# Two softmax attentions: the residual added by TensorE through the identity matrix, the sum copied into x by ScalarE

## Chip, cores and metric

The kernel runs on one core of one Trainium2 chip. The metric is the device time of one execution in microseconds; lower is better. Time before is the median of three runs.

## What is computed

Four transformer layers on x of shape (16, 64, 128), each an attention and a feed-forward part, each with a layer norm in front and a residual add behind. The change touches the attention of layer 0 and that of layer 3. Both are, cut to what matters:

```python
q, k, v = LN(x) @ Wq.T + bq, ctx @ Wk.T + bk, ctx @ Wv.T + bv     # 16 heads of 8
attn = softmax(q k.T / sqrt(8) [+ bias, masked, in layer 3], axis=-1)
x = x + ((attn @ v) @ Wo.T + bo)
```

Behind layer 0's attention comes a mixture of experts (`moe0`), behind layer 3's a quantised feed-forward part (`ffn3`). Each begins with the layer norm of the new x.

## The kernel before

The 1024 tokens are eight tiles of 128. x lies in SBUF as `x_tm` (128 partitions of tokens, tile, 128 features), in float32, for the whole kernel. Every engine runs its own instructions in the order of the program text; semaphores tie the engines together. A piece of text under `@block.scalar` is appended to ScalarE's queue, and so on, so what stands later in the text on the same engine runs later on it.

`attention` (line 449) serves both layers (`masked` is true in layer 3). Its loops run over a step t, with the tiles staggered:

- TensorE (lines 560 to 577), step t: scores of tile t+1 (16 matmul records, line 525) into PSUM banks 0 to 3; transposes of the probabilities of tile t-1 (line 539); values weighed by the probabilities of tile t-2, and the sums of the probabilities (lines 552 and 556); the output projection of tile t-3 (line 576) into bank 7. In layer 3 the values come ahead of the transposes. The values of tile j wait until `o_fm` of tile j-1 is written, the projection of tile j until `o_fm` of tile j is written and until x has taken tile j-1 (`y_added`), as both use bank 7.
- ScalarE (lines 581 to 592), step t: the exponential of tile t, and two copies of the transposed probabilities of tile t-1 from PSUM (line 591). It has nothing to do in the last steps.
- VectorE (lines 611 to 667), step t: reads the scores of tile t (layer 0: maximum, line 636, and difference, line 639; layer 3: scale, bias and maximum, lines 623 to 629); reciprocal of the sums and product into `o_fm` for tile t-3 (lines 656 and 658, in layer 3 also 653 and 654); the add of the projection of tile t-4 into `x_tm` (line 664); the norm's statistics of tile t-5 (line 245).
- GpSimd adds the row bo to all of x once (line 501, in layer 3 line 601), and in layer 3 takes the maximum off the scores (line 605).

The few lines around the projection and the add:

```python
pe.wait_ge(of_ready, j + 1)
if j >= 1:
    pe.wait_ge(y_added, j)
PE.matmul(ps[:, 7, 0:128], o_fm[:, j * P:j * P + P], mat(wo), start=True, stop=True)\
    .then_inc(y_ready, 1)
...
dve.wait_ge(y_ready, j + 1)
V.tensor_tensor(x_tm[:, j], x_tm[:, j], ps[:, 7, 0:128], ALU.add).then_inc(y_added, 1)
```

After the loop of layer 0, ScalarE's queue holds two operations for layer 1 (line 1022, 128x1024 each), and then those of the layer norm: a dummy square root that brings its table in (line 281), the square root of the variance (line 283), which waits for VectorE's statistics (lines 263 and 265), and three of the eight normalised tiles (line 286). After the loop of layer 3 the layer norm follows at once. The layer norm's transposes on TensorE (line 309) wait for the normalised tiles.

SP's queue issues the transfers. `rest_in` counts eleven of them and is waited for only as a whole (`REST`); the transfer of `wq8` is one of them. The weights of layer 2's experts (`moe2_in`, four transfers) go out after layer 0, the mask and bias of layer 3 (`bias_in`, three transfers) after layer 2's attention.

Of the kernel before, what the change touches and what calls it, by code (L numbers as in the profile page):

```python
# [114 lines left out]
def build(nc, A, out):  # L115

    ctx = ExitStack()
    with ctx:
# [109 lines left out]
        V4_CLEAR, KV_CLEAR, AB_CLEAR, V4_CLEAR_AGAIN = 1, 2, 3, 4  # L228

        table, table_set = sb("table", [P, 2]), sem("table_set")  # L230

        @block.gpsimd
        def _(pool):
            G.memset(table[:], 1.0).then_inc(table_set, 1)
            G.memset(v4[:], 0.0).then_inc(cleared, 1)
# [11 lines left out]
        def layernorm(feature_major=True, between=None):  # L247
# [29 lines left out]
            @block.scalar  # L277
            def _(act):
                if n == 0:
                    act.wait_ge(table_set, 1)  # L280
                AC.activation(table[:, 1:2], table[:, 0:1], ACT.Sqrt)
                act.wait_ge(stat_ready, n + 1)
                AC.activation(rstd[:], rstd[:], ACT.Sqrt).then_inc(std_ready, 1)  # L283
                act.wait_ge(shift_ready, n + 1)
                for j in range(ON_DVE, NT):
                    ins = AC.activation(h_tm[:, j, :], x_tm[:, j, :], ACT.Identity, bias=shift[:, j:j + 1],
                                        scale=rstd[:, j:j + 1])
                ins.then_inc(h_rest, 1)
                if between is not None:
                    between(act)  # L290
                if feature_major:

                    for k in range(2):
                        act.wait_ge(tr_ready, 2 * nf + k + 1)
                        AC.activation(h_fm[:, 512 * k:512 * k + 512], ps[:, 4 + k, :], ACT.Copy)\  # L295
                            .then_inc(hf_ready, 1)
# [152 lines left out]
        def attention(n, layer, wq, wo, bo, prepared, masked, bm_ready=None):  # L449
# [56 lines left out]
            def _(pe):  # L506
# [54 lines left out]
                for t in range(NT + 3):  # L561
# [9 lines left out]
                    if 0 <= t - 3 < NT:  # L571
                        j = t - 3
                        pe.wait_ge(of_ready, j + 1)
                        if j >= 1:
                            pe.wait_ge(y_added, j)
                        PE.matmul(ps[:, 7, 0:128], o_fm[:, j * P:j * P + P], mat(wo), start=True, stop=True)\
                            .then_inc(y_ready, 1)

            @block.scalar
            def _(act):  # L580
                for t in range(NT + 2):
# [3 lines left out]
                    if 0 <= t - 1 < NT:  # L585
# [3 lines left out]
                        for k in range(2):  # L589
                            act.wait_ge(ptT_ready, 2 * j + k + 1)  # L590
                            AC.activation(pT[j % 2][:, 512 * k:512 * k + 512], ps[:, 4 + k, :], ACT.Copy)\  # L591
                                .then_inc(pt_ready, 1)

# [14 lines left out]
            def _(dve):  # L608
                if masked:
                    dve.wait_ge(bm_ready, NT)  # L610
                for t in range(NT + 5):
# [47 lines left out]
                    if 0 <= t - 4 < NT:  # L659
                        j = t - 4  # L660
                        if j == 0 and not masked:
                            dve.wait_ge(bo_added, 1)
                        dve.wait_ge(y_ready, j + 1)
                        V.tensor_tensor(x_tm[:, j], x_tm[:, j], ps[:, 7, 0:128], ALU.add).then_inc(y_added, 1)
# [318 lines left out]

        @block.sync
        def _(sp):
            sp.dma_start(l2buf[:, 0:26 * P], A["picks"]).then_inc(rest_in, 16)
# [177 lines left out]
        wq8 = sb("wq8", [P, P], I32)  # L1164
# [5 lines left out]
        def int8_linear(n):  # L1170
# [9 lines left out]

            @block.sync
            def _(sp):
                sp.dma_start(wq8[:], A["wq8"]).then_inc(rest_in, 16)
# [520 lines left out]
        bias_in, bm_ready, bm_done = sem("bias_in"), sem("bias_seen"), sem("bias_ready")  # L1704
# [103 lines left out]
        def _(sp):  # L1808
            sp.wait_ge(x_done, 5)
            sp.dma_start(masks, A["attn_mask"].rearrange("(j p) k -> p j k", p=P)).then_inc(bias_in, 16)  # L1810
            for b in range(2):
                sp.dma_start(bias[S * b:S * b + S].rearrange("p (h k) -> p h k", h=H),
                             A["attn_bias"].rearrange("h q k -> q h k")).then_inc(bias_in, 16)
# [10 lines left out]
        def beside_experts(dve, e):  # L1824
# [10 lines left out]
            if e == 3:  # L1835
# [3 lines left out]
                dve.wait_ge(bias_in, 48)  # L1839
# [281 lines left out]
```

## Time and profile before

| | us |
|---|---|
| median of 3 runs (lowest, highest) | 545.14 (543.63, 546.23) |
| the profiled execution | 544.76 |
| its span, from first to last instruction | 543.0 |
| TensorE matmul busy | 399.5 (74%) |
| VectorE busy | 389.7 (72%) |
| ScalarE busy | 230.0 (42%) |
| GpSimd busy | 130.3 (24%) |
| mean granted TensorE clock | 0.83 of 2.4 GHz |

How to read it: busy time is a mean over stages with different limits, so a stage is read from the timeline and from the chain of work that ended last. In the chain, each piece of time is put down to the instruction that released the next one. Times in the timelines are in us from the start of the span. The granted clock is 1.00 at 2.4 GHz and 0.50 at 1.2 GHz; between these it is the mean of a stretch.

### The profile page before, as it was taken

The page shows a single profiled execution, that of the slowest core. Times are in us where ns is not written, and L with a number is a line of the kernel's source. Part 1 is how long each engine was busy: PE and PEld are TensorE (multiplying, and loading weights), DVE is VectorE, ACT ScalarE, POOL GpSimd, SP SyncE. Part 2 cuts the span into 40 slices and gives each one's busy share as a digit, 9 for nine tenths or more (in the row PEclk, how much of TensorE's full clock was granted, in tenths as well). Part 3 has the DMA queues.
Part 4 walks back from the last instruction along what each step waited for, and adds up shares of the span by engine and source line. Part 5 has one row for each costly group of instructions (what it writes and reads, how often), then busy time and mean ns, then how long its engine had stood idle before and what let it go on. Part 6 is the DMA issues. An engine that isn't in the chain of part 4 may idle for free.

```text
span 543.0 us, 8324 instructions
## 1 busy us (share of the span) xinstructions
PE 399.5 (74%) x3262; PEld 256.8 (47%) x3262; DVE 389.7 (72%) x827; ACT 230.0 (42%) x390; POOL 130.3 (24%) x79
## 2 busy tenths in 40 slices
PE   4998699999999385557798836999933597748016
PEld 2466365666666253323454416677732254633006
DVE  4878446475455868655788975588996999866974
ACT  3655543222223332245687823633603143424931
POOL 2100000039800000059703332000594344100000
PEclk9789799999999557686999986999986558768657
DMA  7950000000000700000000002000000000000001
GB/s 260 355 174 3 0 1 1 1 0 1 0 2 0 309 4 1 1 1 0 1 1 1 2 1 56 4 1 0 1 0 1 2 1 1 2 0 1 0 0 40
DMA packets 11067, 16.69 MB, mean 31 GB/s; under 512 B 5258, under 2 KB 9748, under 8 KB 10132
## 3 DMA queue, kind: packets, MB, share of 16 engines
q1 hardware_dynamic: 10740, 15.37, 8.2%
q10 hardware_dynamic: 288, 0.79, 0.4%
q8 instruction: 26, 0.43, 0.3%
q14 instruction: 13, 0.11, 0.1%
HBM read 15.63 MB, written 0.52 MB: 30 GB/s over the span
## 4 chain that ended last, share of the span: by engine, by line
PE 49%; DVE 38%; ACT 6%; issue 5%; DMA 1%; DVEq 0%; ACTq 0%
PE ps L829 7%; PE ps L834 6%; PE ps L844 6%; PE ps L1764 3%; DVE l2buf L1850 3%; PE ps L1773 3%; PE ps L1929 2%; PE ps L1461 2%; PE ps L525 2%; DVE arena L1617 2%; DVE arena L626 2%; PE ps L1475 2%; PE ps L309 2%; PE ps L539 2%; DVE arena L623 2%
## 5 line engine op out<-in xcount | busy, mean ns | idle before, releaser
L915 DVE SCALAR_TENSOR_TENSOR arena<-ps,cols,arena 128x512 f32<-128x512 f32 x40 | 29.8, 750 | 48.6 <-PE ps L834 46.6
L880 ACT ACTIVATE arena<-ps,cols 128x512 f32<-128x512 f32 x40 | 27.5, 687 | 69.7 <-PE ps L829 69.7
L1617 DVE TENSOR_SCALAR arena<-ps 128x512 f32<-128x512 f32 x56 | 36.7, 684 | 13.4 <-PE ps L1461 9.3
L844 PEld LDWEIGHTS ps<-weights,arena 128*128 128x128 f32 x320 | 38.6, 192 | 8.6 <-issue 8.5
L844 PE MATMUL ps<-weights,arena 128*128 128x128 f32 x320 | 39.2, 276 | 0.2 <-DVE x_tm L904 0.2
L829 PE MATMUL ps<-h_fm,weights 128*128 128x512 f32 x80 | 38.8, 609 | 0.0
L834 PE MATMUL ps<-h_fm,weights 128*128 128x512 f32 x80 | 37.6, 592 | 0.0
L1858 POOL TENSOR_TENSOR l2buf<-l2buf,arena 128x1024 f32<-128x1024 f32 x8 | 25.3, 3193 | 47.1 <-DVE l2buf L1850 47.1
L1461 PE MATMUL ps<-l2buf,picks_b 128*128 128x256 bf16 x160 | 27.2, 299 | 8.4 <-DVE arena L1617 5.1
L584 ACT ACTIVATE arena<-arena 128x1024 f32<-128x1024 f32 x16 | 16.9, 1058 | 34.2 <-POOL arena L605 26.9
L525 PE MATMUL ps<-kexp,q_fm 32*64 32x256 f32 x256 | 28.0, 509 | 4.5 <-DVEq L493 2.4
L1773 PEld LDWEIGHTS ps<-weights,arena 128*128 128x128 f32 x256 | 29.7, 192 | 3.3 <-issue 3.3
L309 PE MATMUL ps<-const,h_tm 128*128 128x128 f32 x48 | 10.3, 385 | 26.6 <-DVE h_tm L271 26.6
L1790 ACT ACTIVATE arena<-ps 128x512 f32<-128x512 f32 x32 | 19.1, 597 | 25.1 <-PE ps L1764 25.1
L1773 PE MATMUL ps<-weights,arena 128*128 128x128 f32 x256 | 29.7, 275 | 0.0
L1764 PE MATMUL ps<-h_fm,weights 128*128 128x512 f32 x64 | 28.7, 594 | 0.7 <-ACT h_fm L295 0.7
L539 PE MATMUL ps<-const,arena 128*128 128x128 f32 x128 | 24.1, 350 | 5.2 <-DVE arena L647 5.2
L605 POOL TENSOR_TENSOR arena<-arena 128x1024 f32<-128x1024 f32 x8 | 17.8, 2231 | 34.2 <-DVE arena L629 34.2
L971 POOL TENSOR_TENSOR wn<-wn,winv 128x1152 f32<-128x1152 f32 x1 | 2.1, 2128 | 96.8 <-DVE winv L961 96.8
L591 ACT ACTIVATE arena<-ps 128x512 f32<-128x512 f32 x32 | 17.9, 594 | 17.3 <-PE ps L539 17.2
L283 ACT ACTIVATE rstd<-rstd 128x8 f32<-128x8 f32 x8 | 1.7, 208 | 54.5 <-DVE rstd L265 54.5
L539 PEld LDWEIGHTS ps<-const,arena 128*128 128x128 f32 x128 | 19.4, 181 | 11.3 <-DVE arena L647 6.0
(327 smaller groups left out, 916.5 us busy)
## 6 DMA issues: line engine op xcount, KB each, us to landing
weights<-in_moe_w SPq DMA_DIRECT2D x2, 2048.0 KB, 10.2
weights<-in_moe_w SPq DMA_DIRECT2D x3, 1280.0 KB
l2buf<-in_picks SPq DMA_DIRECT2D x1, 1664.0 KB, 8.2
rows<-in_rows SPq DMA_DIRECT2D x1, 1216.0 KB, 13.9
x_tm<-in_x SPq DMA_DIRECT2D x2, 256.0 KB, 5.0
ctx_fm<-in_ctx_fm ACTq DMA_DIRECT2D x1, 512.0 KB, 5.7
ctx_tm<-in_ctx SPq DMA_DIRECT2D x1, 512.0 KB, 14.7
mats<-in_mats SPq DMA_DIRECT2D x1, 512.0 KB, 14.8
```

The lines of the kernel that those rows point to most:

```text
L525: ins = PE.matmul(ps[64 * b:64 * b + 64, 2 * (t % 2) + g % 2, 256 * (g // 2):256 * (g // 2) + 256], q_fm[32 * g:32 * g + 32, t * P + 64 * ...
L539: ins = PE.transpose(ps[:, 4 + k, 128 * c:128 * c + 128], prob[j % 3][:, (4 * k + c) * 128:(4 * k + c + 1) * 128], ident)
L829: PE.matmul(ps[:, k, :], w1[:, e, P * k:P * k + P], h_fm[:, t], start=True, stop=True)\
L834: PE.matmul(ps[:, 2 + k, :], w2[:, e, P * k:P * k + P], h_fm[:, t], start=True, stop=True)\
L844: ins = PE.matmul(ps[:, 4 + u % 2, P * t:P * t + P], glu[:, u % 2, k, P * t:P * t + P], w3[:, e, k, :], start=(k == 0), stop=(k == 1))
L880: AC.activation(silu[:, k, :], ps[:, k, :], ACT.Silu, bias=bias_col(0, e, k)).then_inc(silu_ok, 1)
L915: V.scalar_tensor_tensor(out=glu[:, u % 2, k, :], in0=ps[:, 2 + k, :], scalar=bias_col(1, e, k), in1=silu[:, k, :], op0=ALU.add, op1=ALU.m ...
L1461: ins = PE.matmul(ps[:, m % 3, 256 * i:256 * i + 256], picks_b[:, 2 * c + i, :], ixm[:, hg, 256 * half:256 * half + 256], start=True, stop ...
L1617: V.tensor_scalar(hat_rows(u, c), ps[:, m % 3, :], 0.0, 1.0, ALU.max, ALU.min).then_inc(near_ok, 1)
L1764: PE.matmul(ps[:, k, :], m2w1[:, e, P * k:P * k + P], h_fm[:, 0:T2], start=True, stop=True)\
L1773: ins = PE.matmul(ps[:, 4 + e % 2, P * j:P * j + P], hid[:, e % 2, k, P * j:P * j + P], m2w2[:, e, k, :], start=(k == 0), stop=(k == 3))
L1858: G.tensor_tensor(seen_bias[:, j], seen_bias[:, j], over(pen[:, j], 1, H), ALU.add)\
```

## The change

In both attentions the projection of a tile stays open, and a second matmul, with the identity as stationary matrix and x's tile as moving one, adds x to it in PSUM. ScalarE copies the sum over x's tile, in step t for tile t-4, behind the two copies of the probabilities. VectorE's add is gone. TensorE waits for bo's add before the first projection of layer 0, in VectorE's place. Beside it, the transfer of `wq8` moves ahead of three others in SP's queue, and two semaphores are merged into others (`table_set` into `cleared`, `bias_in` into `moe2_in`, for which SP waits once more).

```diff
                         if j >= 1:
                             pe.wait_ge(y_added, j)
-                        PE.matmul(ps[:, 7, 0:128], o_fm[:, j * P:j * P + P], mat(wo), start=True, stop=True)\
-                            .then_inc(y_ready, 1)
+                        elif not masked:
+                            pe.wait_ge(bo_added, 1)
+                        PE.matmul(ps[:, 7, 0:128], o_fm[:, j * P:j * P + P], mat(wo), start=True, stop=False)
+                        PE.matmul(ps[:, 7, 0:128], ident, x_tm[:, j, :], start=False, stop=True).then_inc(y_ready, 1)
 
             @block.scalar
             def _(act):
-                for t in range(NT + 2):
+                for t in range(NT + 4):
...
+                    if 0 <= t - 4 < NT:
+                        j = t - 4
+                        act.wait_ge(y_ready, j + 1)
+                        AC.activation(x_tm[:, j], ps[:, 7, 0:128], ACT.Copy).then_inc(y_added, 1)
...
-                    if 0 <= t - 4 < NT:
-                        j = t - 4
-                        if j == 0 and not masked:
-                            dve.wait_ge(bo_added, 1)
-                        dve.wait_ge(y_ready, j + 1)
-                        V.tensor_tensor(x_tm[:, j], x_tm[:, j], ps[:, 7, 0:128], ALU.add).then_inc(y_added, 1)
...
         @block.sync
         def _(sp):
+            sp.dma_start(wq8[:], A["wq8"]).then_inc(rest_in, 16)
             sp.dma_start(l2buf[:, 0:26 * P], A["picks"]).then_inc(rest_in, 16)
...
-            @block.sync
-            def _(sp):
-                sp.dma_start(wq8[:], A["wq8"]).then_inc(rest_in, 16)
...
             sp.wait_ge(x_done, 5)
-            sp.dma_start(masks, A["attn_mask"].rearrange("(j p) k -> p j k", p=P)).then_inc(bias_in, 16)
+            sp.wait_ge(moe2_in, 64)
+            sp.dma_start(masks, A["attn_mask"].rearrange("(j p) k -> p j k", p=P)).then_inc(moe2_in, 16)
...
-                dve.wait_ge(bias_in, 48)
+                dve.wait_ge(moe2_in, BIAS_IN)
```

## Rows read from the trace of the kernel before

**Rows 1.** The page: the chain that ended last, shares of the span by engine.
```profile
PE 49%; DVE 38%; ACT 6%; issue 5%; DMA 1%; DVEq 0%; ACTq 0%
```
**Rows 2.** Groups by shape (count | busy, mean ns); last: the chain (start, us, what).
```profile
L591 ACT ACTIVATE arena<-ps 128x512 f32<-128x512 f32 x32 | 17.9, 594 | 17.3 <-PE ps L539 17.2
...
L1151 ACT ACTIVATE wT<-ps 128x128 f32<-128x128 f32 x1 | 0.3, 277 | 0.1
...
78.85 1.78 PE ps L844 x16
```
**Rows 3.** Timeline, layer 0 (start, us, engine, line, ..., [idle before <-releaser]).
```profile
41.11 0.28 DVE L664 TENSOR_TENSOR x_tm<-x_tm,ps 128x128 f32<-128x128 f32 x1
...
42.99 0.49 PE L576 MATMUL ps<-mats,o_fm 128*128 128x128 f32 x2
...
45.32 0.28 DVE L664 TENSOR_TENSOR x_tm<-x_tm,ps 128x128 f32<-128x128 f32 x1
45.51 0.29 DVE L245 BATCH_NORM_STATS2 stats<-x_tm 128x6 f32<-128x128 f32 x1
45.52 1.10 ACT L591 ACTIVATE arena<-ps 128x512 f32<-128x512 f32 x2 [0.40 <-PE ps L539]
...
46.87 0.49 PE L576 MATMUL ps<-mats,o_fm 128*128 128x128 f32 x2
```
**Rows 4.** Timeline, end of layer 0's attention and the norm behind it.
```profile
52.83 2.37 ACT L1022 ACTIVATE l2buf<-ctx_fm,cols 128x1024 f32<-128x1024 f32 x2
...
55.21 1.28 ACT L281 ACT_TABLE_LOAD   x1
...
56.50 0.20 ACT L281 ACTIVATE table<-table 128x1 f32<-128x1 f32 x1
...
57.80 0.46 PE L576 MATMUL ps<-mats,o_fm 128*128 128x128 f32 x2 [1.25 <-DVE x_tm L664]
58.30 0.29 DVE L664 TENSOR_TENSOR x_tm<-x_tm,ps 128x128 f32<-128x128 f32 x1 [0.44 <-PE ps L576]
...
60.01 0.21 ACT L283 ACTIVATE rstd<-rstd 128x8 f32<-128x8 f32 x1 [3.30 <-DVE rstd L265]
```
**Rows 5.** Timeline, loop of layer 3's attention.
```profile
449.25 1.29 DVE L623 TENSOR_TENSOR arena<-ps,arena 128x512 f32<-128x512 f32 x2 [0.18 <-PE ps L525]
...
455.31 1.10 PE L552 MATMUL ps<-arena,v 128*32 128x64 f32 x32 [2.45 <-DVE o_fm L658]
...
455.48 1.27 DVE L623 TENSOR_TENSOR arena<-ps,arena 128x512 f32<-128x512 f32 x2
...
458.41 1.09 ACT L591 ACTIVATE arena<-ps 128x512 f32<-128x512 f32 x2 [1.92 <-PE ps L539]
...
459.01 1.42 PE L525 MATMUL ps<-kexp,q_fm 32*64 32x256 f32 x16
...
461.69 1.27 DVE L623 TENSOR_TENSOR arena<-ps,arena 128x512 f32<-128x512 f32 x2
```
**Rows 6.** Timeline, end of layer 3's attention and the norm behind it.
```profile
471.55 0.89 PE L552 MATMUL ps<-arena,v 128*32 128x64 f32 x32 [0.26 <-ACT arena L591]
...
473.59 1.08 ACT L591 ACTIVATE arena<-ps 128x512 f32<-128x512 f32 x2 [2.09 <-PE ps L539]
...
474.69 1.28 ACT L281 ACT_TABLE_LOAD   x1
...
474.73 0.68 PE L552 MATMUL ps<-arena,v 128*32 128x64 f32 x31 [0.58 <-ACT arena L591]
...
478.37 0.29 DVE L664 TENSOR_TENSOR x_tm<-x_tm,ps 128x128 f32<-128x128 f32 x1 [0.44 <-PE ps L576]
...
480.08 0.21 ACT L283 ACTIVATE rstd<-rstd 128x8 f32<-128x8 f32 x1 [3.90 <-DVE rstd L265]
```
**Rows 7.** Stretches of layer 3's loop (length, busy and count by engine, PEclk, DMA).
```profile
452.00:455.00 3.00, 0.81 (x12) 0.25 (x8) 2.93 (x5) 0.03 (x1) 1.87 (x1) 1.00 0.00 0
455.00:458.00 3.00, 2.69 (x52) 2.34 (x53) 2.96 (x6) 1.06 (x1) 0.40 (x1) 0.50 0.00 0
458.00:461.00 3.00, 2.38 (x24) 1.35 (x22) 2.93 (x5) 1.09 (x2) 1.66 (x1) 0.93 0.00 0
```

More of the change, by code:

```diff
@@ L227, in build @@
         cleared = sem("cleared")
-        V4_CLEAR, KV_CLEAR, AB_CLEAR, V4_CLEAR_AGAIN = 1, 2, 3, 4
-        table, table_set = sb("table", [P, 2]), sem("table_set")
+        TABLE_SET, V4_CLEAR, KV_CLEAR, AB_CLEAR, V4_CLEAR_AGAIN = 1, 2, 3, 4, 5
+        table = sb("table", [P, 2])
         @block.gpsimd
         def _(pool):
-            G.memset(table[:], 1.0).then_inc(table_set, 1)
+            G.memset(table[:], 1.0).then_inc(cleared, 1)
             G.memset(v4[:], 0.0).then_inc(cleared, 1)
@@ L279, in _ @@
                 if n == 0:
-                    act.wait_ge(table_set, 1)
+                    act.wait_ge(cleared, TABLE_SET)
                 AC.activation(table[:, 1:2], table[:, 0:1], ACT.Sqrt)
@@ L982, in build @@
         kv = kexp[:].rearrange("p (j h v b d) -> p j h v b d", j=NT, h=H, v=2, b=2)
+        wq8 = sb("wq8", [P, P], I32)
         @block.sync
         def _(sp):
+            sp.dma_start(wq8[:], A["wq8"]).then_inc(rest_in, 16)
             sp.dma_start(l2buf[:, 0:26 * P], A["picks"]).then_inc(rest_in, 16)
@@ L1159, in build @@
         channel_attention(2)
-        wq8 = sb("wq8", [P, P], I32)
         wq8b = sb("wq8b", [P, P], BF16)
@@ L1703, in build @@
         moe2_in = sem("moe2_in")
-        bias_in, bm_ready, bm_done = sem("bias_in"), sem("bias_seen"), sem("bias_ready")
+        BIAS_IN = 64 + 48
+        bm_ready, bm_done = sem("bias_seen"), sem("bias_ready")
         m2w1 = weights[:, 0:4096].rearrange("p (e f) -> p e f", e=NE)
@@ L1809, in _ @@
             sp.wait_ge(x_done, 5)
-            sp.dma_start(masks, A["attn_mask"].rearrange("(j p) k -> p j k", p=P)).then_inc(bias_in, 16)
+            sp.wait_ge(moe2_in, 64)
+            sp.dma_start(masks, A["attn_mask"].rearrange("(j p) k -> p j k", p=P)).then_inc(moe2_in, 16)
             for b in range(2):
                 sp.dma_start(bias[S * b:S * b + S].rearrange("p (h k) -> p h k", h=H),
-                             A["attn_bias"].rearrange("h q k -> q h k")).then_inc(bias_in, 16)
+                             A["attn_bias"].rearrange("h q k -> q h k")).then_inc(moe2_in, 16)
         def free_after_5(eng):
```

## The prediction

> **What bounds the kernel now.** I read the page first, then the groups of instructions by shape for prices. The chain of work that ended last belongs half to TensorE and over a third to VectorE [rows 1]; ScalarE, to which the change gives work, has little of it. So the question is not how busy ScalarE is but where its queue is waited for. The change touches two short stages, the softmax attentions of layer 0 (about 18 to 60 us) and of layer 3 (about 420 to 480 us), so I went to the timeline of each.
>
> In layer 0 the loop over eight tiles runs at VectorE's pace from the third tile on: its add of a tile into x comes every 4.21 us (41.11 to 45.32) [rows 3], and the next instruction follows 0.19 us after the add. TensorE runs the same iteration in 3.87 us (42.99 to 46.86, the two projections) [rows 3] and catches up. The last three tiles are a chain of reciprocal, product and value matmuls in which VectorE and TensorE take turns and the add lies in a gap. The end is: projection of tile 7 at 57.80, add at 58.30, statistics, square root on ScalarE at 60.01 [rows 4]. ScalarE had by then done, in its free tail, two operations for a later layer (line 1022, 52.83 to 55.20) and the load of the square root's table (55.21 to 56.49) [rows 4].
>
> In layer 3 an iteration takes VectorE 6.2 us (455.48 to 461.69, where it starts to read a tile's scores) [rows 5]. TensorE waits 2.45 us for VectorE in it, and ends the scores of the next tile at 460.43, 1.2 us before they are read [rows 5]. Its last tiles hang on ScalarE: twice the value matmuls wait for the copy of the transposed probabilities (471.55 and 474.73) [rows 6].
>
> **The change part by part.**
>
> *The add leaves VectorE.* The add takes 0.28 us, 0.19 of it before the next instruction starts [rows 3]. It can give at most 0.19 x 8 x 2 = 3.0 us. It is on the path only where VectorE paces: tiles at three iterations of layer 0 and three of layer 3, so 0.6 + 0.6 us, if nothing else paces then.
>
> *A second matmul joins each projection.* A float32 128x128 product is two records; sixteen records take 1.78 us at the full clock, 0.11 each [rows 2], so the identity product adds 0.22 us, and about 0.44 at half clock. It lies on TensorE's queue ahead of the next scores. In layer 0 TensorE's iteration becomes 3.87 + 0.22 = 4.09 us.
>
> *The copy to x goes on ScalarE's queue, behind both copies of the transposed probabilities, and the next projection waits for it.* A 128x128 copy out of PSUM takes 0.28 us [rows 2]; two 512-wide ones of 0.594 take 1.10 together [rows 2, 3], so one starts 0.09 before the one ahead ends, and x's is done 0.19 after it. Queued behind the waiting projection are the scores of the tile after next, and in layer 3 also the value matmuls. That is the wait that takes the place of the one on VectorE.
> In layer 0 ScalarE's copies end at 46.62, x would be copied by 46.81, and the projection stood at 46.87 [rows 3]: a stall of 0.0 to 0.1 us. TensorE's pace is then 4.1 to 4.2 us against 4.21 - 0.20 = 4.01 for VectorE. TensorE is late next, and of the 0.6 us some 0.1 is left. I take -0.1 (bounds -0.6 and +0.4).
> In layer 3 the transposes stand directly ahead of the projection, so that nothing covers the copies. Iteration with the projection of tile 2: value matmuls start at 455.31, ScalarE's copies at 458.41, 3.10 us later, for 1.09 [rows 5]. Today the projection runs beside the copies and the scores start at 459.01 [rows 5]. Before this iteration the first projection has been longer at half clock (VectorE already waits 0.18 us on TensorE at 449.25 [rows 5], so +0.4), less one add (-0.2): value matmuls at about 455.6. Then copies 458.7 to 459.8, x at 460.0, projection with identity 0.66 (0.42 + 0.22) until 460.7, scores readable 1.3 of their 1.42 us later, at 462.05. VectorE, which started them at 461.69, would be there at 461.6. So this iteration ends 0.4 late instead of 0.2 early.
> Then the tail. At 471.55 and 474.73 the value matmuls start 0.05 after ScalarE's second copy [rows 6], while the projection ahead of them has been done under it. Now they stand behind x's copy (0.19), a hand-over (0.05) and the projection that waits for it (0.66 at full clock, 1.1 at half): +0.85 each at full clock. The clock was low at the first, so +1.05 there. Layer 3's body: 0.4 + 1.05 + 0.85 = +2.3. Bounds by the clock (rivals): +1.0 and +6.6.
>
> *The end of each stage.* Today the last projection waits for the add of tile 6; the copy of tile 6 will be long done, -0.20. The identity +0.22. Copy in place of add: the same length, plus a hop back to VectorE, +0.05; the statistics of tile 6 are no longer in front, -0.2. By itself, -0.1.
> But ScalarE's work of the free tail now comes behind the last copy. Layer 0: the last copy starts at 58.2 to 58.3; line 1022's two operations start 0.2 later and take 2.37 together, the table 1.28, the small activation and its hand-over 0.2 (all from [rows 4]): 58.25 + 0.2 + 2.37 + 1.28 + 0.2 = 62.3. The square root of 60.01 comes 2.3 us later, and behind it stand the norm and the whole mixture of experts, of which TensorE is the bound: nothing takes it back. The 0.1 of the body is within it. Layer 3 has no line 1022: table and activation, 1.28 + 0.2 behind the last copy, against 1.7 between the add (478.37) and the square root (480.08) [rows 6]. They just end 0.1 late: layer 3 gives +2.3 + 0.1 = +2.4.
> ScalarE's page in the Trainium skill (ScalarE: Activation LUTs, What ACT_TABLE_LOAD costs) gives a table switch about 1.38 us of drain beyond the 1.28. The trace does not show it: the activation starts at 56.50, 0.01 after the load ends [rows 4]. By that rule, the sum would be 1.4 us more in each stage, about 552; I go by the row.
>
> *Edits with one answer.* The wait of the first projection for bo's sum (line 501) is met before it is asked; the wq8 transfer is moved ahead of three others in SP's queue, all counted by one semaphore that is waited for as a whole (the first users come in the mixture of experts); SP's new wait for the layer 2 weights is met before the stage it stands in; merged semaphores keep their order. All 0, since their cover is tens of microseconds.
>
> **Sum.** The profiled execution took 544.76 us (span 543.0), 0.4 under the median of 545.14. 544.76 + 2.3 + 2.4 = 549.46; I say 549.4.
>
> **The rivals.**
> 1. *TensorE's clock stays at 2.4 GHz through layer 3.* Today it changes between the levels: 1.00 of full in 452 to 455, while TensorE was hardly busy, then 0.50 from 455 to 458 after that gap [rows 7]. The change splits the gap of 2.45 us in two of about one microsecond. If the clock stays up, value matmuls and transposes take 2.2 in place of 3.9 us, the loop hides the waits (value matmuls 455.65, projection 459.0 to 459.65, scores readable before 461.6) and of layer 3 there is +1.0 left, the second tail stall with 0.1 each before and behind it. Total +3.3: 548.1. The Trainium skill (TensorE: Matmul & The Clock Gate, Part 1: The HAM clock gate) has the low level as the default and activity as what releases it, which speaks for this rival.
> 2. *The clock is at 1.2 GHz throughout it.* TensorE's iteration is then about 1.9 + 2.9 + 0.9 + 2.3 = 8.0 us against VectorE's 6.0, and layer 3 loses up to 6.6. Total +8.9: 553.7. For it: the value matmuls and transposes of 455 to 458 ran at that level [rows 7]. Against: TensorE would then be nearly without gaps, and it was after such work that it rose (0.93 in 458 to 461) [rows 7].
> 3. *Only the ends cost.* The waits in layer 3 are hidden or given back by the add; +2.3 from layer 0 alone: 547.1.
> 4. *Faster.* If ScalarE's queue at the end of layer 0 is not what the square root waits for (line 1022 placed ahead of the last copies), and the projection never waits for the copy, VectorE's pace decides alone, and six adds of 0.2 go: -1.2, 543.6. It decides if the copies of x end before the transposes of the same iteration do. Against: in both stages today's ScalarE rows stand in the order of the program [rows 4, 6].
> That the change does not do what it says would be the copy leaving ScalarE's queue order, which is rival 4.
>
> **How the numbers follow.** Forecast 0.57, rival 1 0.18, rival 2 0.07, rival 3 0.11, rival 4 0.04, anything else 0.03. The range, 547.2 to 552.0, holds the forecast with the part of rivals 1 and 3 beside it and half way to rival 2; it leaves out rival 4, most of rival 2 and part of rival 3. A measurement of this kernel can tell about 0.5%, 2.7 us, from no change: 547.9. Slower: the forecast, rival 2 and over half of rival 1, less the forecast's own lower tail, 0.79. Same: rival 3 and the rest, 0.18. Faster: 0.03.
>
> **What would show each step.** Right: ScalarE's last 128x128 copy of layer 0 near 58.3 with line 1022's operations and the table load directly behind, and ScalarE's idle before the square root, 3.3 us now [rows 4], gone; the square root at 62.3. Projections of four records that wait for the ScalarE copy in layer 3, the value matmuls of the last two tiles 0.85 or more behind the second copy. Layer 0's iterations at 4.1 to 4.2 us. Wrong: line 1022 ahead of the copies; granted clock in layer 3 at one level throughout; a later stage longer or shorter by more than 1 us, which I have put at nothing.

## The result, and the profile after

The changed kernel takes 551.54 us (median of 8 runs, 547.21 to 556.67) against 545.05 us (median of 8, 543.57 to 546.23). The ratio is 1.009, with a 95% interval from 1.0054 to 1.0126; the ratios in this document leave out runs more than 1.5% above the fastest of their kernel (three here, near 556.5 us, and four of e1), while medians and ranges hold every run. The changed kernel is slower, the direction and the range were right, and the forecast of 549.4 us lies 2.1 under the median. The profiled execution took 551.28 us, 6.5 more than the 544.76 of the kernel before, so its trace can be set against the old one stage by stage.

The page of the changed kernel: the span, the busy time of each engine, and the chain that ended last.
```profile
span 549.5 us, 8389 instructions
...
PE 403.0 (73%) x3294; PEld 260.1 (47%) x3294; DVE 387.2 (70%) x811; ACT 233.2 (42%) x406; POOL 130.4 (24%) x79
...
PE 51%; DVE 34%; ACT 7%; issue 6%; DMA 1%; ACTq 0%; DVEq 0%
```
VectorE's share of the chain fell from 38 to 34% and TensorE's rose from 49 to 51 [rows 1]. The page does not say where. For that I cut both spans at the same instruction, ScalarE's square root in each layer norm (line 283), which stands at the end of every stage. Its starts, subtracted from one another, give this table (us):

| stretch | before | after | difference | forecast |
|---|---|---|---|---|
| up to the first square root | 8.87 | 9.05 | +0.2 | 0 |
| layer 0, softmax attention | 51.14 | 52.60 | +1.5 | +2.3 |
| layer 0, mixture of experts | 118.57 | 119.00 | +0.4 | 0 |
| layer 1, channel attention | 31.85 | 35.32 | **+3.5** | **0** |
| layer 1, int8 stage | 16.56 | 16.57 | 0 | 0 |
| layer 2, attention | 111.93 | 112.16 | +0.2 | 0 |
| layer 2, experts | 72.42 | 72.43 | 0 | 0 |
| layer 3, softmax attention | 68.74 | 71.12 | +2.4 | +2.4 |
| the rest | 62.92 | 61.25 | -1.7 | 0 |

The two stages that the change touches became longer, layer 3 by what was forecast and layer 0 by less. A third, which the diff does not touch, lost more than either.

**Layer 0's end.** The timeline of the changed kernel (start, us, engine, line, operation, out<-in, shapes, in brackets idle before and its releaser):
```profile
57.70 0.28 ACT L598 ACTIVATE x_tm<-ps 128x128 f32<-128x128 f32 x1 [1.17 <-PE ps L579]
57.87 2.36 ACT L1025 ACTIVATE l2buf<-ctx_fm,cols 128x1024 f32<-128x1024 f32 x2
58.01 0.29 DVE L245 BATCH_NORM_STATS2 stats<-x_tm 128x6 f32<-128x128 f32 x1 [0.72 <-ACT x_tm L598]
...
60.25 1.28 ACT L281 ACT_TABLE_LOAD   x1
61.54 0.20 ACT L281 ACTIVATE table<-table 128x1 f32<-128x1 f32 x1
61.65 0.19 ACT L283 ACTIVATE rstd<-rstd 128x8 f32<-128x8 f32 x1
```
This is the queue that was forecast: copy, two operations for layer 1 (line 1022 of before is 1025 here), table load, square root, and no idle time of ScalarE in front of the square root where there were 3.30 us [rows 4].

**Layer 3's tail.** The timeline of the changed kernel:
```profile
477.57 0.60 ACT L593 ACTIVATE arena<-ps 128x512 f32<-128x512 f32 x1 [0.20 <-PE ps L539]
478.06 0.27 ACT L598 ACTIVATE x_tm<-ps 128x128 f32<-128x128 f32 x1
478.48 0.46 PE L578 MATMUL ps<-mats,o_fm 128*128 128x128 f32 x2 [0.94 <-ACT x_tm L598]
478.78 0.39 PE L579 MATMUL ps<-x_tm,const 128*128 128x128 f32 x2
479.09 0.68 PE L552 MATMUL ps<-arena,v 128*32 128x64 f32 x31
```
ScalarE's second 512-wide copy ends at 478.17. The value matmuls started 0.05 behind it before [rows 6]; now they start 0.92 behind it, after x's copy and a projection of four records. In the groups, the projection's idle time in front is:
```profile
L578 PE MATMUL ps<-mats,o_fm 128*128 128x128 f32 x32 | 7.7, 324 | 6.9 <-ACT x_tm L598 5.0 <-DVE o_fm L664 1.8
```

**Layer 1's attention.** TensorE's own timeline, at the scores of the channel attention (256 pairs of weight load and matmul, in two sets of 128; the rows show the matmuls), first of the kernel before:
```profile
183.25 1.54 PE L1100 MATMUL ps<-l2buf,arena 64*32 64x32 f32 x128 [1.73 <-DVE arena L1079]
...
185.65 0.35 PE L1100 MATMUL ps<-l2buf,arena 64*32 64x32 f32 x13 [0.86 <-DVE arena L1079]
...
189.46 1.43 PE L1100 MATMUL ps<-l2buf,arena 64*32 64x32 f32 x115 [3.46 <-issue]
```
and of the changed kernel:
```profile
185.33 1.50 PE L1103 MATMUL ps<-l2buf,arena 64*32 64x32 f32 x125 [1.72 <-DVE arena L1082]
...
192.03 1.63 PE L1103 MATMUL ps<-l2buf,arena 64*32 64x32 f32 x127 [5.20 <-issue]
...
195.85 0.32 PE L1103 MATMUL ps<-l2buf,arena 64*32 64x32 f32 x4 [2.19 <-issue]
```
"<-issue" says that the engine waited for nothing that the profile shows. Before, it did so once, after 141 matmuls, inside the second set; VectorE was working on the first. Now it does so after 125 and again after 252. The first of these lies inside the first set, three matmuls before its end, and VectorE's softmax cannot start without them. The timelines of VectorE, before:
```profile
186.88 0.69 DVE L1124 TENSOR_REDUCE arena<-ps 128x16 f32<-128x512 f32 x1 [0.25 <-DVE x_tm L1081]
```
and after:
```profile
192.38 0.69 DVE L1127 TENSOR_REDUCE arena<-ps 128x16 f32<-128x512 f32 x1 [3.67 <-PE ps L1103]
```
VectorE's softmax starts 8.30 us into the stage before (186.88 less the square root at 178.58) and 11.73 us into it after (192.38 less 180.65). These 3.4 us are the stage's +3.5. TensorE's second stall adds nothing: VectorE takes up the second set 6.7 us after the first in both kernels (15.01 and 18.44 us into the stage), without waiting. Why TensorE stopped is what most of the experiments were about.

### The profile page after: what moved, and what is told of

Same layout as the page of the kernel before. It is cut to its first block, busy times and chain, and to the rows that moved or that the text cites. A ratio compares the mean times of both kernels' runs of the same rounds, so it can differ in the third digit from the quotient of the medians.

```text
span 549.5 us, 8389 instructions
## 1 busy us (share of the span) xinstructions
PE 403.0 (73%) x3294; PEld 260.1 (47%) x3294; DVE 387.2 (70%) x811; ACT 233.2 (42%) x406; POOL 130.4 (24%) x79
## 4 chain that ended last, share of the span: by engine, by line
PE 51%; DVE 34%; ACT 7%; issue 6%; DMA 1%; ACTq 0%; DVEq 0%
PE ps L829 7%; PE ps L834 6%; PE ps L844 6%; PE ps L1763 3%; PE ps L525 3%; DVE l2buf L1850 3%; PE ps L1772 3%; PE ps L539 2%; PE ps L1929 2%; DVE arena L1615 2%; PE ps L1459 2%; PE ps L309 2%; PE ps L552 2%; DVE arena L632 2%; PE ps L1473 2%
## 5 line engine op out<-in xcount | busy, mean ns | idle before, releaser
L834 PEld LDWEIGHTS ps<-h_fm,weights 128*128 128x128 f32 x80 | 15.3, 192 | 19.5 <-issue 19.5
```

The lines of the kernel that those rows point to most:

```text
L834: PE.matmul(ps[:, 2 + k, :], w2[:, e, P * k:P * k + P], h_fm[:, t], start=True, stop=True)\
```

## The experiments

Theory: +2.3 from ScalarE's queue at layer 0's end, +2.4 from the wait for the copy in layer 3, and +3.5 because 32 more TensorE instructions (8 identity products, each a weight load and a matmul in two records) push the points at which TensorE waits for its next instructions onto work that VectorE waits for. Rivals for the last: the transfer of 4 MB of weights that runs in those microseconds alone, the moved wq8 transfer and merged semaphores, and chance.

**e1_tail: ScalarE's free-tail work goes back ahead of the last copies.** The changed kernel, with the two operations of line 1025 and the load of the square root's table placed in the loop.
```
+                    if t == 3 and not masked:
+                        values_l1(act, 0)
...
                     AC.activation(x_tm[:, j], ps[:, 7, 0:128], ACT.Copy).then_inc(y_added, 1)
+                    if t == NT + 1:
+                        if not masked:
+                            values_l1(act, 1)
+                        AC.activation(table[:, 1:2], table[:, 0:1], ACT.Sqrt)
```


> The changed kernel, but ScalarE does the two operations for layer 1 and the load of the square root's table earlier: one in step 3 of layer 0's loop, the other and the load between the copies of x of tiles 5 and 6. Theory 1 (the work of ScalarE's free tail was pushed behind the last copy and costs 2.2 us in layer 0): the square root after layer 0's attention waits for VectorE again and comes 2.2 to 2.4 us earlier than the 52.6 us after the first square root of the changed kernel, at about 50.3; the one after layer 3's attention 0.1 to 0.2 us earlier within its 71.1 us. Rival (the cost lies in the longer projections and TensorE's clock, not in the queue): layer 0 stays at 52 to 53 us. By theory 1 the median is about 2.3 us under the changed kernel's 551.5.

Layer 0 took 50.32 us, 2.28 less than in the changed kernel. Its timeline:
```profile
57.83 0.28 ACT L611 ACTIVATE x_tm<-ps 128x128 f32<-128x128 f32 x1 [0.99 <-PE ps L590]
58.00 0.19 ACT L281 ACTIVATE table<-table 128x1 f32<-128x1 f32 x1
59.45 0.21 ACT L283 ACTIVATE rstd<-rstd 128x8 f32<-128x8 f32 x1 [1.26 <-DVE rstd L265]
```
The last copy is where it was (57.83 to 57.70); the square root follows 1.62 behind it in place of 3.95. That shows the first term, and all fourteen profiles of this study agree on it: from the last write of x to the square root it is 3.95 or 3.96 us in the six with the changed kernel's order, 1.63 in e1, e5 and e11, and 1.71 or 1.72 in the five kernels without the change. Layer 3 stayed at 71.39, but that figure is read too high by the mark in front of it, as shown under e5 and e11. The median is 548.74 us, ratio 1.0032 [0.9994, 1.0069]. This run's profiled execution was an unusual one, 541.42 us. It had its layer 1 at 30.63 us, without a stall after 125 matmuls, though with 4.33 us after 252: the first stall is not there every time.

**e2_first: x's copy goes ahead of the copies of the probabilities.** One block moved up in ScalarE's loop.
```
+                    if 0 <= t - 4 < NT:
+                        j = t - 4
+                        act.wait_ge(y_ready, j + 1)
+                        AC.activation(x_tm[:, j], ps[:, 7, 0:128], ACT.Copy).then_inc(y_added, 1)
                     if 0 <= t - 1 < NT:
```


> The changed kernel with one order turned round: in each step ScalarE copies x's tile before, not after, the two copies of the transposed probabilities. Theory 1 (in layer 3 the projection waits for that copy, and the next scores and value matmuls stand behind it, +2.4 us): the projections of layer 3 no longer wait for ScalarE, the stretch between the square roots around layer 3's attention goes from 71.1 us back to 68.5 to 69.2, and the waits of about 1.0 us at the second matmul's line are gone. Rival (the identity matmuls alone make it longer, each by 0.2 to 0.4 us on TensorE's queue): it stays above 70.5. Layer 0's stretch stays within 0.3 us by both.

Layer 3 took 68.04 us, 3.1 less than the changed kernel and 0.7 less than before. Its tail:
```profile
475.16 0.39 PE L578 MATMUL ps<-mats,o_fm 128*128 128x128 f32 x2
...
475.88 0.28 ACT L590 ACTIVATE x_tm<-ps 128x128 f32<-128x128 f32 x1
476.04 0.68 PE L552 MATMUL ps<-arena,v 128*32 128x64 f32 x31 [0.28 <-ACT arena L597]
```
The projection waits for nothing, and the value matmuls wait for the probabilities alone. The median is 547.12 us, 1.0033 [1.0009, 1.0058]. So in this profile the second term is gone; e5 and e11 say more on its size.

**e3_late_weights and e4_before_late_weights: the 4 MB of weights one stage later,** in the changed kernel and in the one before.
```
-            sp.wait_ge(x_done, 2)
+            sp.wait_ge(x_done, 3)
             sp.dma_start(m2w1...
```


> The changed kernel, with the transfer of layer 2's expert weights (4 MB) let go one stage later, after layer 1's attention. Theory 2 (in layer 1's attention TensorE stands still without a semaphore, 5.2 and 2.2 us, as a block of its instructions is fetched behind this transfer): the first stall of 5.2 us is gone or under 1.5, the stretch of layer 1's attention goes from 35.3 to 28 to 31 us, the median drops by 4 us or more, and the runs scatter by under 3 us in place of 9.5. Rival (the stall belongs to the block boundary and not to the transfer): both stalls stay, 34 to 36 us, and the scatter too.

> The kernel before with the same transfer one stage later, as the partner of the run above. Theory 2: its stall of 3.5 us goes as well, the stretch of layer 1's attention from 31.9 to 28 to 31 us, equal within 0.7 us to that of the run above, and the difference of the two medians is what the attentions cost alone, 4 to 5 us, less than the 6.5 of the first comparison. Rival (layer 1's 3.5 us were chance): the median difference between the two is still 6 to 7 us.

In the changed kernel the stretches around the stall (length, busy and count of PE, PEld, DVE, ACT, POOL, then PEclk, DMA share, GB/s) are:
```profile
186.00:188.00 2.00, 0.83 (x84) 0.69 (x68) 1.97 (x3) 0.00 (x0) 0.00 (x0) 0.50 0.98 418
188.00:190.00 2.00, 0.00 (x0) 0.00 (x0) 0.71 (x1) 0.00 (x0) 0.00 (x0) 0.50 0.98 418
```
The data queues are full. With the weights later they stand at a share of 0.00 to 0.03, and e3's timeline has the stalls in the same places, the first one shorter:
```profile
188.81 1.63 PE L1103 MATMUL ps<-l2buf,arena 64*32 64x32 f32 x127 [1.82 <-issue]
...
192.64 0.32 PE L1103 MATMUL ps<-l2buf,arena 64*32 64x32 f32 x4 [2.19 <-issue]
```
5.20 became 1.82 us and the stage 31.94. In e4 the one stall went from 3.46 to 0.75 us and the stage stayed at 31.82: there it was hidden. Both stages had been expected at 28 to 31 us. So the transfer lengthens the first stall, but neither makes nor places it. In e3 VectorE's softmax starts 8.35 us into the stage, as in the kernel before; a first stall of 1.8 us is short enough to lie under VectorE's other work. In the times none of this arrives. e3's profiled execution is 3.2 us under that of the changed kernel, but its median is 550.75 us (4 runs, 1.0132 [1.0086, 1.0178]), no better than the changed kernel's 1.009, where I had expected at least 4 us less, and it scatters over 5.2 us; e4's is 544.79, 0.9996 [0.9974, 1.0017], so that the two medians still differ by 6.0 us and not by 4 to 5. What takes e3's gain away is open.

**e6_before_pad, e10_before_pad8 and e9_after_pad8: the place of the stall by itself.** Matmuls that nobody reads are put in front of the channel attention: 16 in the kernel before (64 instructions), 8 in it (32 instructions, as many as the change adds), and 8 in the changed kernel. The output is not touched.
```
+                for _ in range(8):
+                    PE.matmul(ps[:, 7, 384:512], ident, const[:, 0:128], start=True, stop=True)
                 pe.wait_ge(wq_ok, 1)
                 pe.wait_ge(x_done, n)
```


> The kernel before with 16 float32 identity matmuls (64 more instructions for TensorE, as many as the change adds) into an unused part of PSUM, where TensorE waits for the end of the mixture of experts, ahead of layer 1's attention. Theory 3 (the longer stall in layer 1's attention comes from the place of the block boundary in TensorE's instructions): the 3.5 us stall of before becomes a pair of about 5 and 2 us, and the stretch of layer 1's attention goes from 31.9 to 34 to 35.5 us; the attentions of layers 0 and 3 stay at 51 and 68.7. Rival (the stall has to do with the time at which the stage begins): the stretch stays at 31.9 plus at most 0.5.

> The kernel before with 8 such matmuls, 32 instructions, exactly as many as the change adds up to this place. Theory 5: the block ends at the 125th and the 253rd record, as in the changed kernel, the stall of 4 to 5 us falls into the first set and a second of about 2 us behind it, the stretch of layer 1's attention goes from 31.9 to 33.8 to 35.5 us and the median rises by 2 to 3.5 us to 547 to 548, with both attentions that the change touches as before. Rival: 31.9 plus at most 0.5 and a median of 545.

> The changed kernel with 8 float32 identity matmuls (32 more instructions for TensorE) into an unused part of PSUM, where TensorE waits for the end of the experts, ahead of layer 1's attention. Theory 5 (TensorE's instructions come in blocks of 256; a block is fetched behind the transfer of the expert weights; the change's 32 instructions of layer 0 moved the block's end from the 141st to the 125th of the 256 score records of layer 1, out of the second set of 128, where VectorE works meanwhile, into the first, for which VectorE waits): 32 more put the ends at the 109th and the 237th; the late block is then the second one, as in the run of before with 64 more, the stretch of layer 1's attention goes from 35.3 to 31.5 to 32.5 us, and the median drops by about 2 to 3.5 us to 548 to 549.5. Rival (the stall has to do with the time, not the place): the stretch stays above 33.8.

e6 came first, and its theory failed: the stage stayed at 31.57 us with one stall of 3.08, as its rival had said. Its 64 instructions are those of the whole change, but only the 32 of layer 0 stand ahead of this stage. So the next two were made with 32. The kernel before with 8 matmuls, e10:
```profile
183.60 1.50 PE L1102 MATMUL ps<-l2buf,arena 64*32 64x32 f32 x125 [1.87 <-DVE arena L1079]
...
190.03 1.63 PE L1102 MATMUL ps<-l2buf,arena 64*32 64x32 f32 x128 [4.92 <-issue]
...
193.86 0.32 PE L1102 MATMUL ps<-l2buf,arena 64*32 64x32 f32 x3 [2.20 <-issue]
```
The changed kernel with 8, e9:
```profile
193.02 1.37 PE L1105 MATMUL ps<-l2buf,arena 64*32 64x32 f32 x108 [0.86 <-DVE arena L1082]
...
197.47 0.43 PE L1105 MATMUL ps<-l2buf,arena 64*32 64x32 f32 x20 [3.08 <-issue]
```

| kernel | instructions ahead of the stage, beyond before | stalls in the 256 matmuls come after | layer 1, us | median, us |
|---|---|---|---|---|
| before | 0 | 141 | 31.85 | 545.05 |
| changed, and e10 | 32 | 125 and 252 or 253 | 35.32, 35.02 | 551.54, 547.22 |
| e9 and e6 | 64 | 236 or 237 | 31.10, 31.57 | 549.19, 544.19 |

The first 32 instructions ahead move the stall 16 pairs earlier, from 141 to 125. Two stalls lie 127 or 128 pairs apart, which is 254 to 256 weight loads and matmuls. With 64 the points are therefore about 109 and 237, and TensorE stops only at the second. e10 contains nothing of the change, and its stage is 3.2 us longer; its median is 3.0 above that of e6, which does twice the extra work (ratios 1.0041 [1.0014, 1.0068] and 0.9996 [0.9977, 1.0015]). VectorE's side agrees in all fourteen profiles: the softmax starts 8.3 or 8.4 us into the stage where there is no long stall in the first set, and 10.8 to 11.7 us in the six where there is. That settles the third term: the change pays for the number of its instructions, by where it puts the next 256 of them. e9 gives the stage back in the changed kernel, and its ratio is 1.0071 [1.0039, 1.0103]; its one profile lost as much in the experts, of which more below.

What is waited for is in the trace. Its DMA view has a queue of kind "instruction", whose packets I looked for in windows of a quarter of a microsecond. In the changed kernel there is none from 180 us to 189.5, and then one (queue: packets, MB, share of the window's 16 engines), at 189.75 to 190:
```profile
q8 instruction: 1, 0.02, 23.9%
```
TensorE, stopped since 186.83, goes on at 192.03. The next comes at 193.0 to 193.25, and the stall of 193.66 ends at 195.85. In the kernel before one comes at 187.25 and its stall ends at 189.46; in e3 they come at 186.25 and 190.0, and its stalls end at 188.81 and 192.64: each time TensorE goes on 2.0 to 2.9 us after such a packet. With no data in the way, e3 enters a block at 188.81, runs it in 1.63, and has the next at 192.64, 3.8 us after entering.

Which stalls are missing is read from the packets too, and here the packets are measured and the reason is argued. Ahead of the scores TensorE waits for ScalarE and VectorE, and a packet that comes before or during these waits costs nothing. This is e11, below, in the stretch 175 to 176 us, before the scores begin:
```profile
q8 instruction: 1, 0.02, 8.3%
```
So it is in e6 (175), in e9 (181) and in e1 (177), and none of these four has the stall in the first set. In e6, e9 and e11 the extra matmuls run there, and the point where one block of instructions ends and the next begins lies among them. In the kernel before, by the same count, a block ends at 13 and another at 141, and the packet of 187.25 is that for 141. The changed kernel, e2, e3, e5, e7, e8 and e10 end a block at 125 and have no packet between 156 us and 186. They all stop there, though by the count the block began three pairs before the scores, ahead of the last of these waits. e1 alone ends a block at the same place with its packet in time. So what calls for a packet is not shown, and why e1 differs is open.

**e5_tail_first and e11_best: both orders mended, and then the stall moved too.** e5 is e1 and e2 together, e11 adds e9's eight matmuls.
```
+                    if 0 <= t - 4 < NT:
+                        j = t - 4
+                        act.wait_ge(y_ready, j + 1)
+                        AC.activation(x_tm[:, j], ps[:, 7, 0:128], ACT.Copy).then_inc(y_added, 1)
                     if 0 <= t - 1 < NT:
...
+                        AC.activation(table[:, 1:2], table[:, 0:1], ACT.Sqrt)
...
+                for _ in range(8):
+                    PE.matmul(ps[:, 7, 384:512], ident, const[:, 0:128], start=True, stop=True)
```


> The changed kernel with both orders of ScalarE's queue mended: the work for layer 1 and the table load in free places of the loop, and x's copy ahead of the copies of the probabilities. Theory 1: both attentions then keep the gain of the add that VectorE no longer does: layer 0's stretch 50.0 to 50.5 us, layer 3's 67.8 to 68.3, against 51.1 and 68.7 of before. Layer 1's attention decides the rest (30.6 to 35 us so far). Median 541.5 to 545, at or under the kernel before; the runs scatter by under 5 us. Rival (the identity matmuls themselves are the cost): both stretches above those of before and the median above 546.

> The changed kernel with both orders of ScalarE's queue mended, and the 8 matmuls of the two runs above. If theories 1 and 5 hold together, nothing of the cost is left: layer 0's stretch 50.4, layer 1's attention 31.5 to 32, layer 3's 68 to 70.5 us, and the median 541.5 to 543.5, 1 to 3 us under the kernel before. If the layer 1 stretch stays at 35, 545.

| kernel | layer 0 | layer 1 | layer 3 | median, us | ratio |
|---|---|---|---|---|---|
| e5 | 50.52 | 35.08 | 70.48 | 545.07 | 1.001 [0.9993, 1.0028] |
| e11 | 51.39 | 31.88 | 70.50 | 541.78 | 0.9946 [0.9925, 0.9968] |

**Layer 3 as one sum with layer 2's experts.** e5 had been expected at 67.8 to 68.3 us in layer 3, and 70.5 looks like a miss. It is the mark that moved. Behind the square root that divides the experts of layer 2 from layer 3's attention stands a small VectorE operation (line 268), and then the first normalised tile (line 271). In the kernel before:
```profile
411.82 0.17 DVE L268 SCALAR_TENSOR_TENSOR shift<-mv,rstd 128x8 f32<-128x8 f32 x1
```
and in e10, whose layer 3 is the code of the kernel before:
```profile
413.40 1.78 DVE L268 SCALAR_TENSOR_TENSOR shift<-mv,rstd 128x8 f32<-128x8 f32 x1
```
In e1, e5, e10 and e11 this operation lasts 1.78 us, the tile follows the square root by 2.18 us in place of 0.56, and the experts in front look 2.1 us shorter. Added together the two stretches agree (us):

| kernels | layer 2's experts and layer 3's attention |
|---|---|
| before, e4, e6, e10, e12 (no change) | 141.2 in each |
| changed, e3, e7, e8, e9, e1 (copy behind the probabilities) | 143.6, 143.6, 145.0, 145.1, 142.2, 141.7 |
| e2, e5, e11 (copy ahead) | 140.4, 140.8, 140.8 |

So the order of the copies costs layer 3 in every one of the six profiles, by 0.4 to 3.9 us, and with the order mended the change gains 0.4 to 0.8 us there. The second term is shown. Its size varies, and it is larger in the profiles with the lower granted clock in layer 3, which was 0.66 to 0.67 in e7 and e8, 0.69 in the changed kernel and in e3, 0.72 in e1 and 0.77 in e9.

In e11's timeline the stall is back in the second set:
```profile
186.20 1.37 PE L1114 MATMUL ps<-l2buf,arena 64*32 64x32 f32 x108 [0.86 <-DVE arena L1091]
...
190.65 0.43 PE L1114 MATMUL ps<-l2buf,arena 64*32 64x32 f32 x20 [3.08 <-issue]
```
Eight matmuls that compute nothing take 3.3 us off e5 and make the one version of this study that beats the kernel before, by 0.5%. e11 is 9.8 us under the changed kernel. Whether all three remedies are needed is not shown, as neither e1 nor e2 was run with the eight matmuls alone. Where its 0.5% comes from is not separated. Against the kernel before its profile (543.03 us) has layer 0 0.3 us longer, layer 2's experts and layer 3 together 0.4 shorter, and the last stretch, which the edits do not touch, 2.2 shorter.

**e12_before_rest: the small edits alone** (wq8's transfer moved, semaphores merged) in the kernel before.
```
+            sp.dma_start(wq8[:], A["wq8"]).then_inc(rest_in, 16)
...
-                dve.wait_ge(bias_in, 48)
+                dve.wait_ge(moe2_in, BIAS_IN)
```


> The kernel before with only the small edits of the change: the transfer of wq8 ahead of three others and the two merged semaphores. Every theory so far puts them at nothing: every stretch within 0.7 us of the kernel before, median 544 to 546. Rival: they shift the transfers or ScalarE's start, and the median rises by over 1.5 us.

545.4 us, 1.0003 [0.9984, 1.0022], no stage over 0.7 us off: they cost nothing.

**e7_after_look1 and e8_after_look2: the changed kernel, profiled again,** because its runs scatter over 9.5 us where those of the kernel before scatter over 2.7.
```
    (no edit)
```


> The changed kernel itself, for another profile. Theory 4 (the changed kernel's runs scatter by 9.5 us since layer 3's loop now hangs on TensorE, and so on its clock, which falls and rises at another place in each run): the stretch of layer 3's attention differs from 71.1 us between the profiles, 69.5 to 77, the longer the lower the granted clock in it, while the stretches of the experts and of layers 1 and 2 stay within 0.7 us. Rival: layer 3 stays at 71.1 plus or minus 0.3 in every profile and another stretch moves.

> The changed kernel itself, a third profile, as for the run above: by theory 4 the time of the run follows the length of layer 3's attention; by the rival it follows another stretch.

The two took 551.70 and 556.43 us. Layer 1 was 33.81 and 33.90 us and layer 3 72.54 and 72.67, 1.4 to 1.6 above the first profile; layer 2's attention was 1.8 to 2.0 below it, which is not explained. What sets e8 apart from e7 is the experts of layer 0, 122.78 us against 119.23. e8's stretches there (PE alone: length, busy, PEclk, DMA share, GB/s):
```profile
102.00:104.00 2.00, 2.00 (x10) 0.50 0.01 4
```
and those of the changed kernel's first profile:
```profile
102.00:104.00 2.00, 2.00 (x7) 1.00 0.00 0
```
TensorE is busy in both, but in e8 its granted clock lies at 0.50, the 1.2 GHz level, for about 7 us of a dense stream. Sixteen matmuls of line 844 take 3.78 us there and 2.05 us in the kernel before. Layer 3, on which I had put the whole scatter, does follow its clock as theory 4 says (0.66 to 0.67 here, 0.69 in the first profile), but it gives 1.5 us of it; between the two it differs by 0.1 us, and the experts by 3.6. e9's profile shows the same (experts 122.83 us). Why it falls in some executions and not in others is open, and so is why none of the ten runs of e11 (541.03 to 543.33) shows it.

## Why the prediction was right, and where it was not

- *The chain at layer 0's end: right.* Forecast: from the last copy to the square root 4.05 us in place of 1.71. Measured 3.95 (57.70 to 61.65), which is +2.2 for the forecast +2.3, and e1 shortens the stage by 2.28. The stage became only 1.5 longer in this profile because its loop was short: from the square root in front to the last write of x it took 48.65 us against 49.43 before, -0.8 where -0.1 was forecast. That part moves by itself, between 48.7 and 50.1 us over the fourteen profiles, and in e7 and e8, at 53.32 and 53.87, the stage was 2.2 and 2.7 longer.
- *Layer 0's pace: right.* In the changed kernel two projections lie 4.12 us apart, 4.1 to 4.2 as forecast and 3.87 before:
```profile
43.05 0.46 PE L578 MATMUL ps<-mats,o_fm 128*128 128x128 f32 x2
...
47.17 0.46 PE L578 MATMUL ps<-mats,o_fm 128*128 128x128 f32 x2
```
- *Layer 3: right in its mechanism,* by projections that wait 0.94 to 1.06 us for x's copy, and value matmuls 0.92 behind ScalarE's second copy where 0.85 or more was forecast. That the size agrees, +2.4 for +2.4, is in part luck. Counted from the square root in front, the value matmuls of the last tile but one start 1.75 us later than before (61.96 and 60.21), of which 0.87 is their own longer wait: the loop ahead had cost 0.9 where I had 0.4. The two waits of the tail cost 1.5 together and not 1.9. And other profiles of the same order have +0.4 to +3.9. Two figures of the working are also off: 0.42 + 0.22 is 0.64 and not 0.66, and a wait at the low clock would be 1.29 by my own prices (0.19 + 0.05 + 1.1, less the 0.05 of before) and not 1.05; no value matmul of the tail had it.
- *Rivals 1 and 2 (the clock in layer 3 at one level):* neither, the mean granted clock of the stretch was 0.69. *Rival 3 (only the ends cost):* out by the waits and by the sums above. *Rival 4 (faster):* out by the queue order. The rule of the Trainium skill on the table switch (ScalarE: Activation LUTs, What ACT_TABLE_LOAD costs) would have added 1.4 us to each stage; the activation again started 0.01 after the load's end (60.25 + 1.28 = 61.53, start 61.54).
- *Every other stage at nothing: wrong, and this is the step that failed.* I had named "a later stage longer or shorter by more than 1 us" as what would show it wrong; layer 1 was 3.5 us longer. I priced the identity products by their 0.22 us each and by who waits for them, and not by being 32 more instructions on a queue. The row that should have warned me was in the trace of the kernel before: the 3.46 us "<-issue" inside a stream of back-to-back matmuls. It was hidden, so I did not ask what placed it. Sum with that term: 544.76 + 2.2 + 2.4 + 3.5 = 552.9 against 551.28; the last stretch, 1.7 us shorter, makes most of the difference. The median lies in the stated range although a term of 3.5 us was missing, since layer 0's loop and the last stretch came out shorter in turn: that part is luck.
- *The last stretch* is one of two lengths over the fourteen profiles, 62.9 or about 61 us (60.62 to 61.78), and it follows TensorE's granted clock. The kernel before, 10 to 12 us behind the square root, in a stretch without a gap (PE alone):
```profile
490.00:492.00 2.00, 2.00 (x4) 0.50 0.01 4
```
and the changed kernel at the same distance:
```profile
498.00:500.00 2.00, 2.00 (x5) 0.88 0.00 0
```
11 to 12 us behind the square root the clock is 1.00 in the six profiles with the short stretch and 0.50 in the eight with the long one. The short one is found in the changed kernel, e1, e2, e3, e5 and e11, and in none of the five kernels without the change, but e7 and e8 are the changed kernel too and have the long one. Why the clock rises earlier in some executions is open.

## What to carry to other kernels

When an operation moves to another engine's in-order queue, list what already stood in that queue's free tail: here 2.4 us of early work and 1.3 of table load were free until a late copy came in front of them, and placing them in the loop gave 2.3 us back. Put the copy that the next matmul waits for ahead of the long copies, not behind. Before a stretch between two marks is called longer, see that the mark keeps its distance from the work behind it: here 2.1 us moved across a mark while the sum of the two stretches stayed the same. And where the trace shows TensorE idle "<-issue" inside a dense stream, count the instructions between such places: adding some far ahead moves the stalls, onto work that others wait for, or to a place behind a wait, where they are hidden.

## What the runs showed of the hardware

- **A dense stream of small matmuls outruns TensorE's instructions.** The matmuls are 32 columns wide and 12 ns apart (125 in 1.50 us), a block of 256 instructions lasts 1.6 us, and the next came 3.8 us after entering it with the data queues idle (e3): a stall of 2.19. The second stalls of the changed kernel, e2, e5, e7, e8 and e10 were 1.92 to 2.47. With 4 MB of weights coming in at 418 GB/s the stalls were 3.08 (e6) to 5.20 us. The Trainium skill (Runtime: NRT & Kernel Launch, Instruction fetch mechanics) says that each engine's instructions come in blocks of 256 by a DMA queue of its own, and that crossing from one to the next is mostly hidden. The trace agrees on the 256 (stalls after 125 and 253 pairs in e10) and has a queue of kind "instruction"; on the hiding it agrees where the packet comes while TensorE waits for others, and disagrees inside this stream. No row says which engine a packet is for; that those named are TensorE's is read from their times.
- **TensorE's granted clock can fall to 1.2 GHz inside a busy stream,** in some executions of the same kernel: 0.50 in e8 at 102 to 106 us where the first profile of the same kernel has 1.00, and 3.6 us on that stage. It can also rise at different times in the same work: the last stretch is 1.1 to 2.4 us shorter where it rises earlier.
- **Stages vary by themselves, and so do marks:** layer 0's loop took 48.7 to 50.1 us, with or without the change. Layer 2's experts and layer 3 each seem to have two lengths 2.1 us apart in kernels in which they are the same code (72.4 and 70.3, 68.74 and 70.96), and their sum is 141.2 us in all five. That is why each claim on a stage here rests on its rows, and each on the total on the medians of many runs.
